# One expert layer's edge scores: a scatter, a load and a scan in place of a lookup, and a new order of the work around it

## The reference

```
h = (x @ W_gat).reshape(M, 4, 4)
a_src = (h * att_src).sum(-1);  a_dst = (h * att_dst).sum(-1)
e = leaky_relu(a_src[src] + a_dst[dst], 0.2)          # dst: an edge's target
ee = exp(e - segment_max(e, dst)[dst])
alpha = ee / (segment_sum(ee, dst)[dst] + 1e-16)
agg = segment_sum(h[src] * alpha[:, :, None], dst) + b_gat
scores = layernorm(agg).reshape(M, 4, 4).mean(1)
w, i = softmax(top2(scores))
out = sum over 4 experts of gate * (gelu(x @ W1 + b1) @ W2 + b2)
```

## Time and profile before

| | |
|---|---|
| three runs | 4207.6, 4210.85 (median), 4214.59 us |
| profiled execution, its own time | 4212.08 us |
| its span in the profile | 4210.3 us |
| busy | PE 3549.8 (84%), DVE 3011.6 (72%), ACT 1491.1 (35%), POOL 1434.7 (34%) |
| expert layer 0 and 1 | about 1240 to 2606, and 2850 to 4210 us |

### The profile page before, as it was taken

How to read it: one execution, slowest core, us unless ns; L and a number is a source line. 1 busy time by engine, 2 the same in 40 slices (tenths; PEclk the granted TensorE clock), 3 DMA queues, 4 the chain that set the end, 5 groups by cost and what they waited for, 6 DMA issues and landing times. The chain is left out here.

```text
span 4210.3 us, 51761 instructions
## 1 busy us (share of the span) xinstructions
PE 3549.8 (84%) x17914; PEld 2021.5 (48%) x17914; DVE 3011.6 (72%) x6268; ACT 1491.1 (35%) x2073; POOL 1434.7 (34%) x1016
## 2 busy tenths in 40 slices
PE   5999999999967987887799994685997878799996
PEld 2333333333325653555465652474753555565654
DVE  2676677667648887778988156867797779888257
ACT  2565555556543520122243420222530112233421
POOL 2776666667650000007730511000000006740520
PEclk9999999999986998888799997786999988899998
DMA  3000000000006300001131347126310001131247
GB/s 141 11 31 11 21 31 21 11 31 31 21 24 221 115 37 16 26 26 37 33 54 56 107 181 291 47 71 210 139 47 11 25 21 41 33 45 40 78 185 290
DMA packets 144857, 301.60 MB, mean 72 GB/s; under 512 B 20580, under 2 KB 103140, under 8 KB 139492
## 3 DMA queue, kind: packets, MB, share of 16 engines
q1 hardware_dynamic: 98212, 180.78, 12.0%
q10 hardware_dynamic: 25920, 94.38, 5.8%
q0 software_dynamic: 20480, 23.14, 3.6%
HBM read 183.42 MB, written 114.81 MB: 71 GB/s over the span
## 5 line engine op out<-in xcount | busy, mean ns | idle before, releaser
L1097 PE MATMUL l_pu<-l_tt,l_w 128*128 128x512 f32 x2048 | 1004.4, 616 | 34.7 <-ACT l_hid L1288 21.7
L1108 PE MATMUL l_pd<-l_w,l_hid 128*128 128x256 f32 x4096 | 968.8, 380 | 9.6 <-ACT l_hid L1288 9.6
L1108 PEld LDWEIGHTS l_pd<-l_w,l_hid 128*128 128x128 f32 x4096 | 782.2, 191 | 328.9 <-issue 246.8
L1288 ACT ACTIVATE l_hid<-l_pu,l_b 128x512 f32<-128x512 f32 x512 | 350.3, 687 | 1306.8 <-PE l_pu L1097 1298.1
L389 DVE TENSOR_TENSOR at_pr<-at_ps,at_decay 128x1024 f32<-128x1024 f32 x512 | 601.1, 1217 | 182.6 <-PE at_ps L503 181.5
L1042 POOL DMA_INDIRECT l_g<-hs_rows,l_i_src x336 | 391.6, 1165 | 905.1 <-DVE l_i_src L1658 803.3
L307 ACT ACTIVATE at_ab<-at_pr 128x1024 f32<-128x1024 f32 x512 | 537.1, 1055 | 436.3 <-DVE at_pr L389 400.4
L258 POOL TENSOR_TENSOR at_ab<-at_ab 128x1024 f32<-128x1024 f32 x256 | 600.9, 2372 | 180.6 <-ACT at_ab L307 180.6
L1097 PEld LDWEIGHTS l_pu<-l_tt,l_w 128*128 128x128 f32 x2048 | 400.2, 199 | 334.5 <-issue 312.8
L503 PE MATMUL at_ps<-at_qr,at_kr 32*128 32x512 f32 x2048 | 348.9, 644 | 14.5 <-issue 9.5
L522 PE MATMUL at_ps_av<-at_pr,at_v 128*32 128x512 f32 x2048 | 281.5, 612 | 7.3 <-ACT at_o L315 5.1
(11 more groups left out here) (341 smaller groups left out, 4189.0 us busy)
## 6 DMA issues: line engine op xcount, KB each, us to landing
ys<-l_yst ACTq DMA_DIRECT2D x112, 512.0 KB, 2.6
l_yb<-ys SPq DMA_DIRECT2D x28, 2048.0 KB, 9.9
l_tt<-tT ACTq DMA_DIRECT2D x36, 512.0 KB, 3.4
at_xt<-in_x SPq DMA_DIRECT2D x16, 1024.0 KB, 5.1
l_xt<-x SPq DMA_DIRECT2D x32, 512.0 KB, 4.1
tT<-l_xnT ACTq DMA_DIRECT2D x32, 512.0 KB, 4.5
l_xo<-x SPq DMA_DIRECT2D x28, 512.0 KB, 4.3
x<-at_xt SPq DMA_DIRECT2D x8, 1024.0 KB, 4.3
```

Source lines behind the costliest of these rows:

```text
L1097: ins = pe.matmul(ps_u[q % 2][:, :], w1[:, e, c, P * q:P * q + P], tt[:, s, c, :], start=(c == 0), stop=(c == KK - 1))
L1108: ins = pe.matmul(out, hid[:, k % 2, c, P * r:P * r + P], w2[:, k % GE, c, :], start=False, stop=(c == MB - 1), skip_group_check=True)
L1288: act.activation(hid[:, k % 2, q, :], ps_u[q % 2][:, :], ACT.Gelu, bias=b1[:, k % GE, q:q + 1]).then_inc(s_act, 1)
```

## The change

- **Scores.** `is_col`, its products and sums are gone. `targets()`, called right behind `sort()`, computes the run ends in two halves, and for each of the 64 target tiles the first slot of its run. POOL scatters the score of each tile's target to that slot, 64 indirect DMAs into four DRAM tensors `spots` (one wait each for the one four back), ahead of the 168 gathers. SP loads the four tensors (344 KB each) into `spot`; DVE masks each by its slot's owner, sums the four, and one scan spreads each score over its run. The four tensors are filled with zeros at the layer's start by four DMAs.
- **Order.** The first exchange unit comes ahead of all four rounds (`ROUNDS1 = 0`), a round is 14 steps, the late part 20; in the loop the unit comes first and all 68 steps behind it.
- **Clamped terms.** The merging of L1708 to L1729 is done in the loop, behind the DMA to `found`, its exponential on ACT at `IN_CLAMPED = 12`.
- **The powers.** POOL's two go: `rstd2` is a square root on ACT and a reciprocal on DVE, the other an exponential on ACT, both written between ACT's steps of the last eight pairs.

```diff
-ROUNDS1 = 2
+ROUNDS1 = 0
-PRE_ROUND = 11
+PRE_ROUND = 14
-PRE_LATE = 14
+PRE_LATE = 20
-IN_FRONT = 18
-IN_SCAN = 20
-IN_MERGE = 52
+IN_SCAN = 6
+IN_CLAMPED = 12
+IN_MERGE = 36
@@ SP
+            for k in range(SPOTS):
+                sp.dma_start(spots_v[k], blanks).then_inc(s_blanks, 16)
...
+                for k in range(SPOTS):
+                    sp.wait_ge(s_put[k], m * (16 * NT // SPOTS) + 16 * NT // SPOTS)
+                    sp.dma_start(spot[:, k, :, :].rearrange("p j h -> p (j h)"), spots_v[k]).then_inc(s_spot, 16)
@@ POOL
+                for c in range(NT):
+                    k, before = c % SPOTS, c // SPOTS
+                    if before:
+                        pool.wait_ge(s_put[k], m * (16 * NT // SPOTS) + 16 * before)
+                        pool.sem_inc(s_pgo, 1)
+                    pool.indirect_dma_start(spots[k][:, :], bass.IndirectOffsetOnAxis(ap=i_row[:, 0, 1, c:c + 1].bitcast(U32), axis=0),
+                                            ad[:, c, :], None).then_inc(s_put[k], 16)
...
-            pool.wait_ge(s_var, 1)
-            pool.tensor_tensor(rstd2, var, nhalf, ALU.pow).then_inc(s_rstd, 1)
-            pool.wait_ge(s_dif, 1)
-            pool.tensor_tensor(v2, euler, v1, ALU.pow).then_inc(s_ex, 1)
@@ PE
-                experts(IN_FRONT, PRE_PAIRS, PRE_PAIRS + LOOPED, m)
...
-                experts(4 * LOOPED + 4 - IN_FRONT, PRE_PAIRS, PRE_PAIRS + LOOPED, m)
+                experts(4 * LOOPED + 4, PRE_PAIRS, PRE_PAIRS + LOOPED, m)
@@ ACT
+                loop(IN_CLAMPED)
+                act.wait_ge(s_e0, m + 1)
+                act.activation(ye[:, :, :, :], ym[:, :, :, :], ACT.Exp).then_inc(s_p0, 1)
...
-            experts(4 * (PAIRS - PRE_PAIRS - LOOPED) + 4, PRE_PAIRS + LOOPED, PAIRS, LAST)
+            experts(2, PRE_PAIRS + LOOPED, PAIRS, LAST)
+            act.wait_ge(s_var, 1)
+            act.activation(deviation, var, ACT.Sqrt).then_inc(s_rstd, 1)
+            experts(3, PRE_PAIRS + LOOPED, PAIRS, LAST)
+            act.wait_ge(s_dif, 1)
+            act.activation(v2, v1, ACT.Exp).then_inc(s_ex, 1)
+            experts(4 * (PAIRS - PRE_PAIRS - LOOPED) - 1, PRE_PAIRS + LOOPED, PAIRS, LAST)
@@ DVE, in the loop
-                then(dve.tensor_tensor(is_col, cb[:, :].unsqueeze(2).to_broadcast([P, JT, NT]),
-                                       iota_ps[:, 0:NT].unsqueeze(1).to_broadcast([P, JT, NT]), ALU.is_equal))
-                for h in range(GH):
-                    for q in range(JT // LOOK):
-                        cols = slice(LOOK * q, LOOK * q + LOOK)
-                        then(dve.tensor_tensor(prod, is_col[:, cols, :],
-                                               ad_ps[:, :, h].unsqueeze(1).to_broadcast([P, LOOK, NT]), ALU.mult))
-                        then(dve.tensor_reduce(adj[:, h, cols], prod, AX.X, ALU.add))
...
+                dve.tensor_copy(keeps[:, :, :], keep[:, 0, :].unsqueeze(1).to_broadcast([P, GH, JT]))
+                dve.tensor_scalar(pen[:, :, :], keep[:, 0, :].unsqueeze(1).to_broadcast([P, GH, JT]), -1.0, 1e30, ALU.add, ALU.mult)
+                then(dve.tensor_tensor(own[:, :, :], slot_of[:, 0, :].unsqueeze(2).to_broadcast([P, JT, SPOTS]),
+                                       iota_ps[:, 0:SPOTS].unsqueeze(1).to_broadcast([P, JT, SPOTS]), ALU.is_equal))
+                dve.wait_ge(s_spot, m * (16 * SPOTS) + 16 * SPOTS)
+                for k in range(SPOTS):
+                    ins = dve.tensor_tensor(owned[:, k, :, :], spot[:, k, :, :], own[:, :, k].unsqueeze(2).to_broadcast([P, JT, GH]), ALU.mult)
+                then(dve.tensor_reduce(starts, owned.rearrange("p k j h -> p h j k"), AX.X, ALU.add))
+                then(dve.tensor_tensor_scan(*(a.rearrange("p h j -> p (h j)") for a in (adj[:, :, :], keeps[:, :, :], starts)), 0.0, ALU.mult, ALU.add))
@@ DVE, behind the loop
+            then(dve.reciprocal(rstd2, deviation))
```

More of the change, by code:

```diff
@@ L803, in ffn_layer @@
             tmp = sb("tmp", [P, MTT, GF])
-            code = sb("code", [P, EC], I32)
+            with ExitStack() as coded:
+                code = tensors(coded)("code", [P, EC], I32)
+            with ExitStack() as sorted_:
+                sb = tensors(sorted_)
+                g = sb("g", [P, JT, HSW])
+                raw = sb("raw", [P, JT], I32)
+                order = sb("order", [P, JT], I32)
+                i_src = sb("i_src", [P, JT], I32)
+                cf = sb("cf", [P, JT])
+                cb = sb("cb", [P, JT], BF16)
+                keep = sb("keep", [P, 2, JT])
+                ge = sb("ge", [P, NT + 1])
+                has = sb("has", [P, NT])
+                at_row = sb("at_row", [P, 2, NT])
+                i_row = sb("i_row", [P, 2, 2, NT], I32)
+                work = sb("work", [P, NT // 2, JT], BF16)
+                slot_of = sb("slot_of", [P, 2, JT])
             nodes.close()
@@ L826, in ffn_layer @@
             res = sb("res", [P, NT, ROWW])
-            cb = sb("cb", [P, JT], BF16)
-            keep = sb("keep", [P, JT])
             pen = sb("pen", [P, GH, JT])
[L830 to L834, removed]
+            keeps = sb("keeps", [P, GH, JT])
+            own = sb("own", [P, JT, SPOTS])
             adj = sb("adj", [P, GH, JT])
@@ L839, in ffn_layer @@
             xe = sb("xe", [P, 2, GH, JT])
[L840 to L848, removed]
+        spot = pay[:, :, :].rearrange("p k j -> p (k j)").rearrange("p (k j h) -> p k j h", k=SPOTS, h=GH)
+        owned = rows[:, :, :].rearrange("p j c -> p (j c)")[:, 0:SPOTS * JT * GH].rearrange("p (k j h) -> p k j h", k=SPOTS, h=GH)
+        starts = xm[:, 0, :, :]
+        fac = keeps
+        blanks = sent[:, :, :, :].rearrange("p a c j -> p (a c j)").bitcast(F32)[:, JT * GH // 2:JT * GH // 2 + JT * GH]
+        tm = new[:, :, :]
         flat_rows = rows[:, :, :].rearrange("p j c -> p (j c)")
@@ L887, in ffn_layer @@
         s_fnd = [sem(f"fnd{k}") for k in range(ABREAST)]
+        s_put = [sem(f"put{k}") for k in range(SPOTS)]
+        s_blanks, s_first, s_spot = sem("blanks"), sem("first"), sem("spot")
         def landed(n, group, k):
@@ L1668, in _ @@
             sort()
+            targets()
+            turn_to_next()
             rounds(ROUNDS1, ROUNDS0)
@@ L1705, in _ @@
             dve.wait_ge(s_last, 16)
[L1706 to L1711, removed]
@@ L1800, in _ @@
                 sort()
+                targets()
+                dve.wait_ge(s_p0, m + 1)
+                dve.sem_inc(s_go, 1)
+                then(dve.tensor_tensor(ye[:, 1, :, :], ye[:, 1, :, :], over(count[:, :], GH), ALU.mult))
+                then(dve.tensor_tensor(den, den, ye[:, 0, :, :], ALU.mult))
+                for h in range(GH):
+                    cols = slice(GH + GE * h, GH + GE * h + GE)
+                    dve.tensor_tensor(state[:, :, cols], state[:, :, cols], ye[:, 0, :, h:h + 1].to_broadcast([P, NT, GE]), ALU.mult)
+                    ins = dve.tensor_tensor(sum2[:, :, cols], last[:, GE * h:GE * h + GE].unsqueeze(1).to_broadcast([P, NT, GE]),
+                                            ye[:, 1, :, h:h + 1].to_broadcast([P, NT, GE]), ALU.mult)
+                dve.tensor_copy(den2, ye[:, 1, :, :])
+                dve.memset(count[:, :], 0.0)
+                then(dve.memset(cz[:, :], 0.0))
+                then(dve.tensor_tensor(state[:, :, :], state[:, :, :], sum2[:, :, :], ALU.add))
                 for k in range(ABREAST):
@@ L2147, in build @@
     more = dram("more", (P, MORE), I32)
+    spots = [dram(f"spots{k}", (P * JT + P, GH)) for k in range(SPOTS)]
     consts = {n: a[n] for n in ("ident", "first", "above", "not_above", "places", "iota_row", "part", "iota")}
```

110 lines of the change are left out of this document (61 added, 49 removed).

## The result

The changed kernel takes 4271.47 us (median of 4, 4265.85 to 4279.73) against 4209.27 us before. The ratio is 1.0145, its 95% interval 1.0129 to 1.0161: 1.45% slower, where the prediction said 4264 us and 1.3%.

The account below looks back on a forecast made before the run. PE's expert steps were taken as the bound, so PE's idle times were summed: 16.6 - 3.3 - 2.3 + 4.1 + 11.2 = 26.3 us a layer, 52.6 in two, giving 4264 us; 8-in-10 range 4238 to 4286.

Parts of the forecast that it names:

- The bound: Where DVE does the lookup, PE's expert steps bind, one per 3.45 us; only PE's idle time can change.
- First round: Ahead of the first round, `targets()` adds 26.9 us on DVE against three more PE steps: PE idle 24.9, +16.6 a layer.
- Loop's unit: At the loop's exchange unit, PE's 3.31 us wait for DVE goes as the lookup is gone: -3.3 us a layer.
- Late round: With 20 steps ahead instead of 14, PE's 5.15 us idle shrinks to about 2.8: -2.3 us a layer.
- ACT's turns: In the loop, PE's stall at the exponentials grows from 1.54 to some 3.7, plus 1.9 at `IN_MERGE`: +4.1 us a layer.
- Powers: In the last eight pairs, powers wait their turn on ACT, making the second pair of results late: +11.2 us a layer.
- L: The end of the looped steps, 2441.4 in the trace before, from which the powers' times in the tail are counted.
- Scatters: POOL's 232 indirect DMAs take 356 us, ending about 75 us before DVE asks: slack used, 0 us cost.
- Table loads: On ACT in the tail, 1.28 us each with no drain; by the skill's page the time would be some 6 us higher.
- The zeros: Four 344 KB DMAs at the layer's start are hidden: 0, up to 5 us a layer if they delay block loads.
- all bounds low: The case with the terms' bounds at their low ends (25, 0, 7, 0): a layer loses 16.3 us.

Follow-up runs that it names:

- e6: Kernel before the change without the lookup's sixteen products and sums, on a slower chip: 4749.18 us against 4756.2, ratio 0.9981.
- e2: Changed kernel with seven of the late part's 20 steps moved ahead of the first round (21, 14, 14, 14, late 13): 4232.06 us, ratio 1.0051.
- e1: Changed kernel with both powers back on POOL and out of ACT's program: 4250.71 us, ratio 1.0101.
- e5: Kernel before the change with only the powers moved to ACT, on a slower chip: 4787.21 us against 4756.2, ratio 1.0058.
- e12: Changed kernel with the 64 scatters a layer written twice, on a chip where the kernel before takes 4211 us: 4280.77 us, ratio 1.0164.
- e4: Kernel before the change with the third round at 14 steps instead of 11 and the late part at 11 instead of 14: 4214.39 us, ratio 1.0014.
- e8: Changed kernel with the 64 scatters written three times, one execution on the chip of e5: 5324.33 us.
- e7: Changed kernel with the 64 scatters written twice, one execution on the chip of e5: 5150.31 us.

## Why the prediction was right

- **The bound.** Right: PE's steps bind, and the lookup lies beside them. e6 took 189 us of DVE's work away for 5 to 13 us.
- **First round, +16.6.** 15.75 in layer 0 (24.08 less 8.33) and 16.4 in layer 1. e2 gave it back by putting PE's steps there.
- **Loop's unit, -3.3.** 3.31 to none.
- **Late round, -2.3.** -3.2, with 0.4 more in the second turn: -2.8.
- **ACT's turns, +4.1.** 2.5 in layer 0 (2.80 + 1.21 less 1.54), 4.2 in layer 1 (4.01 + 1.74 less 1.55).
- **Powers, +11.2.** 11.3 in layer 0 and 10.4 in layer 1, as the second pair of results shows, with the square root at L + 16.7 (15.8 predicted), the gates at L + 35.2 (35.4) and PE's stalls 1.58 and 5.41 (7 predicted). e1 gave back 21 us, e5 lost 21 to 34.
- **Scatters, 0 and 75 us of slack.** 79 us, by e12. POOL's scatters and gathers take 354.7 us, from 1798.3 to 2153.0, where 356 were predicted. The scatters' port clash (3.03 us a row under one-hot rows) is in the trace as in the earlier trace rows and cost nothing.
- **Table loads.** The trace of the tail has 1.28 us and the next operation at once (2468.49 behind 2467.20, 2486.03 behind 2484.74), and the term fits. The drain that the Trainium skill adds (ScalarE: Activation LUTs, What ACT_TABLE_LOAD costs) does not show here.
- **The zeros, 0.** PE's first work of the layers stands 20.41 and 20.96 us for a load of the biases, against 21.02 and 20.07 before.

The five terms measured give 12.1 + 11.3 = 23.4 us in layer 0 and 14.5 + 10.4 = 24.9 in layer 1, 48.3 together, where the prediction had 52.6. The span grew by 53.8. From PE's first work in a layer to its last wait for ACT, the layers are 23.8 and 26.3 us longer, so that 1.8 is missing there; the first steps behind the longer idle are slower (5.08 us from one step to the next at 1851.12, against 4.19 at 1953.62 before). The start of layer 0 is 2.1 us earlier, and the end behind layer 1 is 1.0 longer.

The stretch between the two layers, with the end of layer 0 and the convolution, which the change does not touch, is 4.8 us longer. The other runs split it. Up to the first matmul of the convolution it is 69.7 us before and 72.3 after. It is 72.3 to 73.8 in all six kernels with the powers on ACT, e5 on its own chip among them, and 69.0 to 70.8 in all eight with the powers on POOL. So some 3 us more belong to the powers, in a place where the sum had no term for them. The 2.2 behind it, inside the convolution, are not explained, nor are the 8 us by which the medians stand further apart than the profiles.

So that 52.6 comes so near to the 53.8 of the profiles is in part luck: the terms came out 4 us smaller, and 5.5 us came from places that the sum did not have. The sum for its range has a slip as well: with all bounds low a layer loses 16.1 us, not 16.3.

What failed outright is not in the prediction but in the expectations behind it. The prediction's late round spoke of a wait of DVE, and I took it for free to move steps away from it; e2 and e4 showed the length of DVE's chain there.

## What to carry to other kernels

When work is taken from an engine that runs beside the bound, first find the bound's own idle times and what ends each one; only those can be won, and here they were 3.3 us for 95. When a short operation is moved to an engine with a program in fixed order, its price is its place: 0.26 us on ACT cost 11 where 10.6 us on POOL cost nothing. And before judging a change together with a new order of work, give the old kernel the same care: other step counts alone were worth 19 us on it, and the changed kernel, tuned in the same way, came out 11 or 14 us ahead of the kernel before.

## What the runs showed of the hardware that was not expected

The kernel before the change takes 4209 to 4211 us beside all other runs, and 4756 on the chip of e5 to e8, in all 15 executions there. What differs there are the stretches in which POOL issues indirect DMAs back to back. In them POOL keeps its pace, and DVE, PE and ACT come nearly to a stand. In e6, in the stretch of the eights, a DVE operation starts only every 1.4 to 2.1 us:

```profile
1945.16 0.09 DVE L1494 MATCH_VALUE_LOAD l_key<-l_cand,l_key 128x8 f32 x1 [0.28 <-issue]
1946.56 0.42 DVE L1494 MATCH_REPLACE8 l_key<-l_cand,l_key 128x256 f32<-128x256 f32 x1 [1.31 <-issue]
1948.65 0.09 DVE L1494 MATCH_VALUE_LOAD l_key<-l_cand,l_key 128x8 f32 x1 [1.68 <-issue]
...
2083.79 2.29 DVE L1480 TENSOR_TENSOR l_one_lo<-l_iota,l_lo 128x4096 bf16<-128x4096 bf16 x1 [98.94 <-issue]
...
2138.47 2.29 DVE L1480 TENSOR_TENSOR l_one_lo<-l_iota,l_lo 128x4096 bf16<-128x4096 bf16 x1 [51.25 <-remote]
```

PE has one-hot rows to sum in the same time and starts one matmul of 0.21 us in about 2.8 us, for no reason that the profile shows ("issue"). In the window loop, while POOL gathers the ends of the runs, PE and ACT stand for 30 us at a time:

```profile
1987.87 0.21 PE L1161 MATMUL l_ph<-l_one_hi,l_one_lo 128*128 128x64 bf16 x1 [2.58 <-issue]
1990.68 0.21 PE L1161 MATMUL l_ph<-l_one_hi,l_one_lo 128*128 128x64 bf16 x1 [2.60 <-issue]
...
2567.69 3.72 PE L1108 MATMUL l_pd<-l_w,l_hid 128*128 128x256 f32 x8 [30.26 <-issue]
```

```profile
2566.62 0.69 ACT L1288 ACTIVATE l_hid<-l_pu,l_b 128x512 f32<-128x512 f32 x1 [32.90 <-remote]
```

And the windows of e6 (columns as in the earlier trace rows):

```profile
1985.00:2083.00 98.00, 7.63 (x36) 3.61 (x35) 0.00 (x0) 1.20 (x2) 74.22 (x79) 0.50 0.11 8
```

In 98 us POOL issues 79 DMAs, PE does 36 matmuls, ACT two operations and DVE none. Whether DVE waits there for PE's matmuls or is itself held is not told by the trace. The stretch from the first exchange unit to the late round takes 401 us in e6 against 200 in the kernel before on the first chip, the one from ACT's first turn in the loop to the last eight pairs 230 against 158: some 273 us in layer 0, and twice that is the 546 us between the chips.

On such a chip POOL's queue is on the path, and each scatter that the change adds would cost its length: 64 more cost 87 us a layer between e7 and e8, and PE's waits at the histogram with "issue" as their end grow from 619 to 782 us. The Trainium skill (SBUF — State Buffer, Who interferes with whom) has DVE and GpSimd excluding each other on a shared port, and PE and ACT waiting for no one there. POOL's rows of 3.03 us under DVE's one-hot operations fit such a lock, and they are on this chip too (one of 3.03 us at 1981.50 in e6). By the same section of the Trainium skill a `tensor_tensor`, which the one-hot operations are, did not stall a DMA; here the measurement decides. The standstill of PE and ACT is outside that rule, so that the port can't be the whole of what differs. Why it happens was not found, and how much slower the change is on that chip was not measured.
